# Decoder layer on one core: softmax results turned by VectorE blocks and SBUF-to-SBUF transfers instead of TensorE, with the output products behind the next pair's scores

## What is computed

```python
h_q = (x @ w_q.T).reshape(b, lq, H, DH)          # 512 -> 32 heads x 128
h_k = (key_value_states @ w_k.T).reshape(b, lk, H, DH)
h_v = (key_value_states @ w_v.T).reshape(b, lk, H, DH)
score = jnp.einsum('bqhd,bkhd->bhqk', h_q, h_k) + position_bias[None]
score = jax.nn.softmax(jnp.where(m, score, -jnp.inf), axis=-1)
score = jnp.where(m, score, 0.0)
attn = jnp.einsum('bhqk,bkhd->bqhd', score, h_v).reshape(b, lq, H * DH)
out = attn @ w_out.T
```

## Time and profile before

| | us |
|---|---|
| median of 3 runs (lowest, highest) | 924.41 (923.97, 925.29) |
| the profiled execution, its own time | 923.94 |
| its span from first to last instruction | 922.2 |
| PE busy | 873.8 (95%) |
| DVE busy | 627.6 (68%) |
| ACT busy | 424.1 (46%) |
| POOL busy | 353.1 (38%) |
| DMA, mean over the span | 117 GB/s |

### The profile page before, as it was taken

One profiled execution on the slowest core, in us unless ns is written; L12 is line 12 of the kernel. 1 busy time (PEld: TensorE's weight loads), 2 busy tenths in 40 slices (PEclk: granted clock), 3 DMA queues, 4 the chain that ended last, 5 costly groups with the idle time before them and its releaser, 6 DMA issues.

```text
span 922.2 us, 14534 instructions
## 1 busy us (share of the span) xinstructions
PE 873.8 (95%) x4528; PEld 732.2 (79%) x4528; DVE 627.6 (68%) x1086; ACT 424.1 (46%) x1091; POOL 353.1 (38%) x328
## 2 busy tenths in 40 slices
PE   4789998999999999988999999999999999999898
PEld 4677786887677888767888888888888888888697
DVE  6877775677876666566557766676657766676654
ACT  3553344566434435264545453555445553554220
POOL 2312333333443323152764355534464355533100
PEclk9999999999999999999999999999999999999999
DMA  8025665555666767607244442535234441533002
GB/s 273 12 92 136 160 138 137 138 149 137 151 149 158 202 159 138 143 20 193 74 121 116 117 114 79 142 91 142 82 112 122 111 128 68 139 91 68 1 1 92
DMA packets 207661, 108.27 MB, mean 117 GB/s; under 512 B 136592, under 2 KB 187920, under 8 KB 203920
## 3 DMA queue, kind: packets, MB, share of 16 engines
q1 hardware_dynamic: 207632, 107.91, 44.7%
HBM read 74.34 MB, written 33.55 MB: 117 GB/s over the span
## 4 chain that ended last, share of the span: by engine, by line
PE 80%; DVE 10%; issue 3%; POOL 2%; DMA 2%; ACT 2%; SPq 1%; DVEq 0%; ACTq 0%; POOLq 0%
PE bank L575 63%; PE bank L629 6%; PE bank L647 6%; PE bank L639 3%; DVE w_lo L1259 2%; DVE turned L1351 2%; DVE st L1268 1%; DMA values<-turned 1%; PE bank L593 1%; SPq L337 1%; DVE stats L1152 1%; DMA acc<-in_x 1%; POOL w_sum L479 1%; POOL rstd L458 1%; DVE acc L1145 1%
## 5 line engine op out<-in xcount | busy, mean ns | idle before, releaser
L955 ACT COPY st<-bank 128x512 f32<-128x512 f32 x192 | 112.2, 587 | 266.5 <-PE bank L575 260.0
L575 PE MATMUL bank<-ctx_hi,w_hi 128*128 128x512 f32 x448 | 179.7, 401 | 15.6 <-DVE st L1268 7.8
L1268 DVE TENSOR_TENSOR st<-bank,st 128x512 f32<-128x512 f32 x144 | 98.6, 689 | 125.4 <-PE bank L575 125.3
L575 PE MATMUL bank<-ctx_hi,w_lo 128*128 128x512 f32 x448 | 175.4, 391 | 0.0
L575 PE MATMUL bank<-ctx_lo,w_hi 128*128 128x512 f32 x448 | 175.3, 391 | 0.0
L477 POOL TENSOR_TENSOR w_sum<-raw 128x256 f32<-128x256 f32 x48 | 39.6, 825 | 248.8 <-PE bank L575 224.3
L536 POOL TENSOR_TENSOR probs<-probs,row_scale 128x512 f32<-128x512 f32 x64 | 66.6, 1041 | 177.3 <-DVE row_scale L1233 174.3
L575 PEld LDWEIGHTS bank<-ctx_hi,w_hi 128*128 128x128 f32 x448 | 84.4, 188 | 45.5 <-issue 11.0
L575 PE MATMUL bank<-wo_hi,ot_hi 128*128 128x512 f32 x256 | 104.9, 410 | 5.4 <-issue 3.6
L1145 DVE TENSOR_TENSOR acc<-bank,acc 128x512 f32<-128x512 f32 x136 | 93.6, 690 | 20.6 <-PE bank L575 18.7
L901 ACT ACTIVATE probs<-probs,neg_max 128x128 f32<-128x128 f32 x264 | 102.4, 393 | 1.1 <-DVE neg_max L1217 1.1
(11 more groups left out here) (135 smaller groups left out, 1520.2 us busy)
## 6 DMA issues: line engine op xcount, KB each, us to landing
raw<-in_weights SPq DMA_DIRECT2D x128, 256.0 KB, 3.1
values<-turned SPq DMA_DIRECT2D x64, 256.0 KB, 4.3
v<-values SPq DMA_DIRECT2D x64, 256.0 KB, 4.5
keys<-st SPq DMA_DIRECT2D x14, 1024.0 KB, 4.8
st<-keys SPq DMA_DIRECT2D x14, 1024.0 KB, 7.4
acc<-in_x SPq DMA_DIRECT2D x8, 256.0 KB, 7.6
ctx_raw<-in_ctx_t SPq DMA_DIRECT2D x4, 512.0 KB, 9.9
bias<-in_pos_bias SPq DMA_DIRECT2D x16, 128.0 KB, 2.0
```

Source lines behind the costliest of these rows:

```text
L575: ins = pe.matmul(out_ap, lhs[a], rhs[b], start=start and k == 0, stop=stop and k == n - 1, skip_group_check=again)
L955: act.copy(to[:, i, j, :], (y, other, y, y)[which][:, :]).then_inc(act_took, 1)
L1268: dve.tensor_tensor(to[:, i, j, :], (other, y, other)[which][:, :], to[:, i, j, :], ALU.add).then_inc(dve_took, 1)
```

## The change

The softmax results of a head must stand with their keys on the partitions before the value products. Now, for all pairs but the last:
- POOL writes the scaled results into two buffers of half a head, `weighed`, instead of in place.
- DVE turns each half in 32 x 32 blocks (`turn_probs`), back into the buffer of the exponentials. A block stays in its 32 partitions.
- SP moves the 4 x 4 blocks to their partitions with 16 DMAs a head, each of 32 partitions x 1 KB (`move_probs`), into `probs_t[j]`, of which there are now two.
- PE has no transposes in the loop, ACT and DVE no copies of turned results.

The value products of both heads of pair g - 1 move into pair g (head 0 behind slots 0 to 3), and the output products of g - 1 stay behind the scores of g, all eight together at the end of the pair, over six banks (`OUT`) instead of two. DVE's order changes: row scales come ahead of the additions, and the low parts 2 and 3 of the query weights move to the start of the next pair. SP fetches the query weights and bias one pair earlier, and keys between the two heads' moves. The FFN weights are fetched at the end of the first refill, and cast and split in four parts: ACT at the end of pairs 1 to 4, POOL in pairs 2 to 5. The last pair is still turned by PE (`turn_last_probs`, in banks QK), and `copy_last_probs` copies the results to `probs_t[j]`. `fetch_queries(g)`, `next_out(g)` and `next_keys(g)` are the waits and loads of before under new names.

```diff
-        probs_t = put("probs_t", ctx_at + 8 * KB, [P, B, P])
+        probs_t = [put("probs_t1", ctx_at + 8 * KB, [P, 4, B, QUAD]), put("probs_t2", w_at + 22 * KB, [P, 4, B, QUAD])]
+        by_block = [t[:, :, :].rearrange("p b n -> p (b n)").rearrange("p (c b q) -> p c b q", c=4, b=B)
+                    for t in probs]
+        weighed = [put("weighed0", w_at + 26 * KB, [P, HALF, P]), put("weighed1", rows_at + 14 * KB, [P, HALF, P])]
...
+        OUT = VO + TO + SC + VO
...
+            def move_probs(g, j):
+                sp.wait_ge(blocks_turned, 2 * (PAIR * g + j) + 2)
+                if not isinstance(g, int) or g:
+                    sp.wait_ge(pv_done, 2 * PAIR * g + 2 * j)
+                for a in range(4):
+                    for c in range(4):
+                        sp.dma_start(probs_t[j][cols(c, QUAD), a, :, :].rearrange("k b q -> k (b q)"),
+                                     by_block[j][cols(a, QUAD), c, :, :].rearrange("k b q -> k (b q)")
+                                     ).then_inc(probs_t_moved[j], 16)
...
+            sp.wait_ge(product_done, SLOTS * (K1 + 1))
+            move_probs(0, 0)
+            move_probs(0, 1)
+            fetch_queries(2)
+            next_out(1)
+            fetch_bias(2)
...
+            def refill(g, first=False, ahead=2):
 
                 sp.wait_ge(pv_done, 2 * PAIR * g + 2)
                 load_values(g)
-                if not last:
-                    sp.wait_ge(scores_done, 2 * PAIR * g + 6)
-                    load_keys(g + 1)
-                    sp.wait_ge(wo_lo_ready, g + 1)
-                    fetch_out(g + 1)
-            with sp.Fori(1, GROUPS - 1) as g:
+                move_probs(g, 0)
+                next_keys(g + 1)
+                move_probs(g, 1)
+                if ahead == 2:
+                    fetch_queries(g + 2)
+                next_out(g + 1)
+                if ahead == 2:
+                    fetch_bias(g + 2)
+                if first:
+                    fetch_ffn()
...
-            def normalise_probs(g, j):
+            def normalise_probs(g, j, last=False):
                 for i in range(2):
                     pool.wait_ge(scale_ready, 2 * (PAIR * g + j) + i + 1)
-                    pool.tensor_tensor(probs[j][:, half(i), :], probs[j][:, half(i), :],
+                    s = PAIR * g + j
+                    if last and j:
+                        pool.wait_ge(probs_turned, 2 + i + 1)
+                    elif not isinstance(s, int) or s:
+                        pool.wait_ge(blocks_turned, 2 * s - 1 + i)
+                    pool.tensor_tensor(weighed[i][:, :, :], probs[j][:, half(i), :],
                                        row_scale[:, j, half(i)].unsqueeze(2).to_broadcast([P, HALF, P]),
                                        ALU.mult).then_inc(probs_ready, 1)
...
+            for g in range(1, 2 + FFN_PARTS):
+                pair(g, (lambda: low_ffn(g - 2)) if g > 1 else None)
+            with pool.Fori(2 + FFN_PARTS, GROUPS - 1) as g:
                 pair(g)
             pair(GROUPS - 1, last=True)
...
+                if j == 0 and (not isinstance(g, int) or g):
+                    pe.wait_ge(out_added, B * g - 2)
...
-            def turn_head_probs(g, j):
-                pe.wait_ge(ot_lo_ready, 2 * (PAIR * g + j + 1))
-                turn_probs(PAIR * g + j + 1, probs[j])
-            def weigh_head_values(g, j):
+            def weigh_head_values(g, j, last=False):
+                s = PAIR * g + j + 1
                 pe.wait_ge(v_loaded, 64 * g + 64)
-                weigh_values(PAIR * g + j + 1, lambda b: v[:, j, b, :], probs_t)
-            def project_out(g, some):
+                if not last:
+                    pe.wait_ge(probs_t_moved[j], 256 * g + 256)
+                pe.wait_ge(ot_lo_ready, 2 * s)
+                if j == 0:
+                    pe.wait_ge(out_added, B * g + HALF)
+                for i in range(2):
+                    if last:
+                        pe.wait_ge((probs_t0_copied, probs_t1_copied)[i], 1 + j + 1)
+                    for t in range(HALF):
+                        b = HALF * i + t
+                        ins = pe.matmul(TO[i][:, cols(t)], v[:, j, b, :], probs_t[j][:, :, b, :], start=True, stop=True)
+                    ins.then_inc(pv_done, 1)
+            def turn_last_probs(j):
+                for i in range(2):
+                    pe.wait_ge(probs_ready, 2 * (HEADS - 1 + j) + i + 1)
+                    for t in range(HALF):
+                        ins = pe.transpose(QK[i][:, cols(t)], weighed[i][:, t, :], ident[:, :])
+                    ins.then_inc(probs_turned, 1)
+            def project_out(g, some=range(B)):
                 pe.wait_ge(wo_lo_ready, g + 1)
                 for b in some:
-                    if b % HALF == 0:
-                        pe.wait_ge(ot_lo_ready, 2 + 2 * PAIR * g + 3 + b // HALF)
-                    pe.wait_ge(out_added, B * (g + 1) + b - 1)
-                    three_pass(VO[b % 2][:, :],
+                    if b == 0:
+                        pe.wait_ge(ot_lo_ready, 2 + 2 * PAIR * g + 3)
+                        pe.wait_ge(out_added, B * (g + 1))
+                    elif b == 2:
+                        pe.wait_ge(ot_lo_ready, 2 + 2 * PAIR * g + 4)
+                    elif b == 4:
+                        pe.wait_ge(scores_biased, 2 + 2 * PAIR * (g + 2))
+                    elif b >= 6:
+                        pe.wait_ge(out_added, B * (g + 1) + b - 5)
+                    three_pass(OUT[b][:, :],
...
+            def pair(g, first=False, last=False):
                 project_queries(g, range(4))
-                turn_head_probs(g - 1, 1)
+                weigh_head_values(g - 1, 0)
                 project_queries(g, range(4, SLOTS))
 
                 pe.wait_ge(dve_took, 3 * (FIRST + g) + 3)
                 weigh_head_values(g - 1, 1)
                 pe.wait_ge(act_took, 4 * (FIRST + g) + 4)
                 head_scores(g, 1)
-                project_out(g - 1, range(6))
-                turn_head_probs(g, 0)
-                project_out(g - 1, (6, 7))
-                weigh_head_values(g, 0)
+                if last:
+                    project_out(g - 1, range(6))
+                    turn_last_probs(0)
+                    project_out(g - 1, (6, 7))
+                else:
+                    project_out(g - 1)
...
+            def pair(g, then=None, first=False, last=False):
                 n = FIRST + g
 
                 act.wait_ge(scores_done, 2 * PAIR * g + 2)
                 take(n, 0, qt)
                 take(n, 1, qt)
                 take(n, 2, qt)
-                copy_probs_t(PAIR * g, probs_t)
+                if first:
+                    high_out(0)
+                split_head_out(g - 1, 0)
...
-                copy_probs_t(PAIR * g + 1, probs_t)
+                if last:
+                    copy_last_probs(0)
                 act.wait_ge(out_done, B * (g + 1))
                 high_out(g)
-                split_head_out(g, 0)
-            pair(1)
-            act.wait_ge(ffn_loaded, 48)
-            act.copy(ffn[0][:, :], ffn_raw[:, :]).then_inc(ffn_hi_ready, 1)
-            with act.Fori(2, GROUPS - 1) as g:
+                if then is not None:
+                    then()
...
+            for g in range(1, 1 + FFN_PARTS):
+                pair(g, lambda: high_ffn(g - 1), first=g == 1)
+            with act.Fori(1 + FFN_PARTS, GROUPS - 1) as g:
...
+            def turn_probs(g, j, i):
+                if i == 0:
+                    dve.wait_ge(probs_ready, 2 * (PAIR * g + j + 1) + 2)
+                dve.transpose(by_block[j][:, :, half(i), :].rearrange("p c b q -> p b c q"),
+                              weighed[i][:, :, :].rearrange("p b (c q) -> p b c q", c=4)).then_inc(blocks_turned, 1)
...
+            def pair(g, first=False, last=False):
                 n = FIRST + g
+                if not first:
+                    low_for_queries(g, 2)
+                    low_for_queries(g, 3)
                 take(n, 0, qt)
-                copy_probs_t(PAIR * g, probs_t)
+                split_head_out(g - 1, 0)
...
-                for b in range(B):
-                    add_out(g, b)
-                    if b < 2:
-                        row_scales(g, 0, b)
-                    elif b in (2, 3, 4, 6) and not last:
-                        low_for_queries(g + 1, (2, 3, 4, 6).index(b))
-                    if b in (4, 5):
-                        row_scales(g, 1, b - 4)
-                    if b == 5:
-                        copy_probs_t(PAIR * g + 1, probs_t)
-                split_head_out(g, 0)
-            with dve.Fori(1, GROUPS - 1) as g:
+                row_scales(g, 0, 0)
+                row_scales(g, 0, 1)
+                add_out(g, 0)
+                add_out(g, 1)
+                if not last:
+                    turn_probs(g, 0, 0)
+                    turn_probs(g, 0, 1)
+                add_out(g, 2)
+                if not last:
```

(49 more changed lines are left out.)

109 lines of the change are left out of this document (60 added, 49 removed).

## The result

The changed kernel takes 1002.91 us (median of 4 runs, 1001.75 to 1004.06); the kernel before took 924.19 in the same comparison (4 runs, 920.6 to 925.29). The ratio is 1.087, 95% interval 1.084 to 1.0901: 8.7% slower, where 1.0% faster was forecast. The mechanism is the third rival's, the queue of small moves.

A forecast was written before the change was run, and what follows sets the result against it. PE, busy throughout the pair stage, was taken as the bound at 29.53 us a period. 923.94 + 12 - 13 x 1.6 - 0.9 = 914.2, with 0.5 for the median 915 us, 1.0% less; range 903 to 932.

The forecast's parts named there:

- the third rival: Loop and start: the queue of small moves makes the kernel slower from c = 0.50; 943 us at 0.54; chance 0.22.
- c: SP's time for one move's issue: 0.43 us in the loop, 0.47 outside it, bounds 0.38 and 0.75.
- part 3: SP and a head's way in the loop: the 32 moves a pair hide, with 2.2 us to spare or more.
- the prediction's own formula: Loop period if SP sets the pace: 12.9 + 31c us, meeting 27.9 at c = 0.484.
- the 0.7 for late exponentials: Term of the SP-paced loop period: 0.7 us for exponentials that start late.
- Part 1: PE in the loop: without the transposes a period falls by 1.92 us, from 29.53 to 27.61.
- Part 2: DVE in the loop: some 1.0 us more work a period, 0.3 us lost to POOL, so 27.9 us a period.
- Part 4: First two pairs: together 12 us more.
- (a): Pair 0's moves: output products start at about 423.4 instead of 426.4, -3 us, bounds -6 and +3.
- (b): Pair 1: ScalarE waits for FFN weights, next output products at 47.8 us against 32.6, +15.2, bounds +11.7 and +19.4.
- Rival 2: Start: no wait for the FFN weights, if their fetch place was misread; 894.5 us.
- Part 5: Kernel's end: the last pair keeps its transposes, one inside a wait, about 0.9 us saved, bounds 0 and 2.

The follow-up runs named there:

- experiment 1: Kernel before, with seven series of 16 back-to-back transfers of several kinds on SP and one on ScalarE's queue added at its end; 1019.66 us.
- Experiment 9: Changed kernel with 13 of the 16 moves of each head from pair 1 on, the other three left out; 942.86 us, ratio 1.0196 to the kernel before.
- experiment 5: Changed kernel with the raw query weights fetched by ScalarE's queue instead of by SP behind all 32 moves; 996.44 us.
- experiment 8: Kernel of experiment 7 with the third and fourth low parts ahead of DVE's last two additions; 887.34 us, timed again at 890.66 us, ratio 0.9613 to the kernel before.
- experiment 4: Changed kernel with the three FFN weight fetches ahead of the first refill instead of at its end; 988.77 us.
- experiment 7: Changed kernel with the edit of experiment 4 and each head's 16 moves replaced by 4 stores to DRAM and one load; 894.75 us.

## Why the prediction was wrong

**What failed is above all one term, c, in part 3.** The step read "I take c = 0.43 in the loop, since 128 long rows are nearer to 32 than 512 short ones". It ordered the nearest rows by their number of pieces. Between 32 and 128 pieces what decides is whether either end is DRAM (experiment 1): 0.42 us if so, 0.59 if not, and 0.635 from one start to the next in the changed loop. The bounds of 0.38 to 0.75 held it; the value taken did not. With c = 0.635 the prediction's own formula gives 12.9 + 31 x 0.635 = 32.6 us a period, 61 us more in 13 than with 27.9, and its rival 3, at the point c = 0.50 from which it decides, had the sign, the place and the mechanism.

**The formula itself was 1.3 us short.** Measured were 33.9. The period from 685.6 to 719.4 is 5.9 to the first move, 20.3 to the last move's issue (as 31c + 0.6 says), 2.1 to its landing and 5.5 for value products and scores. The prediction priced these at 3.6 us; behind a PE that had waited they ran at a granted clock of 0.6 to 0.8. That is 1.9 more, and the 0.7 for late exponentials did not appear. Experiment 9, where PE hardly waits, comes within 0.5 us of the formula. The raw weights behind the moves add about 0.5 on average (experiment 5, one run).

**Part 1 was right**: 27.61 forecast, 27.65 measured once nothing else was in the way (experiment 8).

**Part 2 was near.** The block transposes cost 664 to 716 ns each, two in 1.30 us, against 0.6 taken. The low parts met POOL as forecast. In the trace of the kernel before, low parts of 128x512 (L1259) took between 0.67 and 2.83 us, the longest at 401.08, beside POOL's mask addition of 2.53 from 400.83; none of the 136 additions with a bank as an input (L1145) took more than 0.69, also not the one at 669.96, inside POOL's 2.18 us from 668.58. In the changed kernel, DVE and POOL in time order:

```profile
698.32 2.37 DVE L1373 TENSOR_TENSOR w_lo<-w_sum,w_hi 128x512 fp32r<-128x512 f32 x1
700.62 2.87 DVE L1373 TENSOR_TENSOR w_lo<-raw,w_hi 128x512 fp32r<-128x512 f32 x1
```
```profile
697.75 2.40 POOL L554 TENSOR_TENSOR wo_lo<-raw,wo_hi 128x1024 fp32r<-128x1024 f32 x1 [1.86 <-ACT wo_hi L1155]
700.11 5.62 POOL L548 TENSOR_TENSOR bias_mask<-mask_add,bias 128x1024 f32<-128x1024 f32 x2
```

POOL's low output weights end at 700.15 and the third part at 700.69; the fourth gets in behind the first of the two masks, as the steps said. The cost is 28.2 - 27.65 = 0.55 us a period and not 0.3, shown by moving the two parts in experiment 8, where it goes in the ten later periods; the rival there, that the parts "only push the additions back", fell for these. DVE's busy time rose by 4.6 us a period and not by 1.0, most of it in the two rows above, which hold 5.2 us where 1.2 is the price alone.

**Part 4 had the mechanism and missed the size.** (a) Output products of pair 1 start at 425.8, 0.6 earlier than before, forecast 3: the 32 straight-line moves took 21.05 us and not 15. (b) 55.4 us where 47.8 was forecast, +22.8 and not +15.2, beyond its bound of +19.4. The last FFN issue starts at t = 455.88 - 425.80 = 30.1 in place of 24.5, again by the moves' price, and its landing of 7.4 took back 0.6; and the two slots behind the wait took 5.2 us and not 2.7, at a granted clock of 0.54, for which the steps had put nothing. Together +22.2 us, not +12. Rival 2 (no wait) is refuted by the 25.50 us of ScalarE's row.

**Part 5 came out**, but proves little: 79.3 us from the last start of the loop's output products to the end before, 78.5 after, -0.8 against -0.9. The same end took 77.4 to 78.7 us in the other runs, and 83.5 in experiment 4.

**The sum by its terms**: 922.2 + 22.2 + 13 x (33.92 - 29.53) - 0.8 = 1000.7 for the span, as measured. Of the error of 88 us, 78 are the period (33.9 in place of 27.9: 61 by c, 17 by the formula) and 10 the start.

The range reached to c = 0.515, and the chances of 0.22 for the third rival and 0.23 for a slower kernel were too low. No row before showed a transfer from SBUF to SBUF, and the bounds of c lay on both sides of the break-even of 0.50; the value in the middle of them, 0.565, would already have forecast a slower kernel.

## What to carry to other kernels

When a change multiplies the number of transfers, price the queue's issue time. Here it went by the kind of transfer before its size, 0.59 us inside SBUF at 32 and at 128 rows of 1 KB and 0.42 with DRAM at one end (experiment 1): find or make a row of the same kind, source and destination both, before taking a value. Put the count into a formula for the period, look where it crosses the engine that is the bound now, and if the unknown price has that point inside its bounds, forecast by the bounds and not by the likeliest row. The way through DRAM is worth a trial where the added landing has slack: here 10 issues a pair in place of 32 inside SBUF took 94 us less (experiment 7 beside 4), and PE waited 0.3 us in the loop for a landing. And where a forecast has PE wait, price the products behind the wait higher than undisturbed ones: value products and scores took 5.5 us here behind a wait of 2.9, at granted clocks of 0.6 to 0.8, and 3.65 in the kernel without moves.

## What was not expected of the hardware

- An issue from SBUF to SBUF occupies its queue for 0.59 us, one with DRAM at either end for 0.42 (0.44 at 128 rows of 2 KB). The first price is the same at 32 and at 128 rows and on SP and ScalarE (10.31 and 10.42 us for 16), and with both queues issuing it hardly moved (6.4 to 6.6 us for ten on SP, 3.9 for six on ScalarE).
- A wait of 2.9 us on PE was followed by some 5.5 us at a granted clock of 0.6 to 0.8, and cost 1.8 us beyond itself; behind a wait of 0.5 us the clock stayed at 1.00. Behind the same wait of 2.58 us at the end of the kernel, 60 products took 8.9 us at a granted clock of 0.91 in the changed kernel and 14.1 us at 0.56 in experiment 4.
- Going through DRAM, 1 MB a pair written and read again with 189 GB/s in all (experiment 7), was some 89 us faster than the same bytes moved inside SBUF in 32 transfers a pair.
- A DVE subtraction of 0.6 us (two in 1.25 in experiment 8, with POOL idle for most of it) took 2.4 to 2.9 beside POOL's work: the third low part was done 0.54 us behind POOL's running instruction. Placing two such instructions ahead of two additions brought 0.55 us a period in the ten later ones and 4.3 us over the loop.
